# Expert blocks of an eight-layer kernel: tokens scattered into slots ahead of the tile loop, weights copied to fixed buffers, f32 matmuls

## What is computed

```python
probs = softmax(x @ gate_w + gate_b)          # [2048, 8]
topw, topi = top_k(probs, 2); topw = topw / topw.sum(-1)
hid = gelu(einsum('nd,edf->enf', x, w1) + b1)  # w1: [8, 128, 512]
out = einsum('enf,efd->end', hid, w2) + b2     # w2: [8, 512, 128]
final = (out * ew * mask).sum(axis=0)          # weights of the chosen experts
```

## Time and profile before

| | |
|---|---|
| median of 3 runs | 1203.41 us (1202.26 to 1234.69) |
| the profiled execution's own time | 1192.77 us |
| its span | 1190.6 us |
| busy: TensorE / VectorE / ScalarE / GpSimd | 846.7 / 674.1 / 507.5 / 226.8 us |
| mean granted clock of TensorE | 0.819 of full |
| the chain that ended last | TensorE 44%, VectorE 17%, issue 10%, ScalarE 10%, GpSimd 8%, unknown queue 5%, DMA 3% |
| DMA | 32.98 MB, 28 GB/s on average |

### The profile page before, as it was taken

One profiled execution on the slowest core, in us unless ns is written; L12 is line 12 of the kernel. 1 busy time (PEld: TensorE's weight loads), 2 busy tenths in 40 slices (PEclk: granted clock), 3 DMA queues, 4 the chain that ended last, 5 costly groups with the idle time before them and its releaser, 6 DMA issues.

```text
span 1190.6 us, 17358 instructions
## 1 busy us (share of the span) xinstructions
PE 846.7 (71%) x5666; PEld 481.4 (40%) x5666; DVE 674.1 (57%) x1340; ACT 507.5 (43%) x1061; POOL 226.8 (19%) x208
## 2 busy tenths in 40 slices
PE   4599644888825547898878888878784787574784
PEld 2377434666614331111111111111564565374663
DVE  6734767111157768669999999960626311574112
ACT  1110431433316353458888888884233233211332
POOL 2000014465511200000000000000302464101562
PEclk9799756899967765559999999995795699785798
DMA  6100210111120000000000000000203111101113
GB/s 161 46 1 1 72 35 10 35 43 41 41 80 1 0 1 1 1 1 1 1 1 1 1 1 1 1 1 1 71 1 106 27 41 37 35 1 35 39 43 93
DMA packets 35946, 32.98 MB, mean 28 GB/s; under 512 B 6898, under 2 KB 28738, under 8 KB 35874
## 3 DMA queue, kind: packets, MB, share of 16 engines
q1 hardware_dynamic: 30434, 20.82, 6.1%
q0 software_dynamic: 5440, 11.15, 3.7%
HBM read 22.18 MB, written 9.76 MB: 27 GB/s over the span
## 4 chain that ended last, share of the span: by engine, by line
PE 44%; DVE 17%; issue 10%; ACT 10%; POOL 8%; another core or an unknown queue 5%; DMA 3%; SPq 2%; DVEq 0%; POOLq 0%; ACTq 0%
PE psum L1331 12%; PE psum L1319 9%; ACT arena L1383 6%; POOL results L891 4%; POOL arena L883 3%; DVE arena L1298 2%; DVE stats L158 2%; PE psum L1283 2%; PE psum L217 2%; PE psum L916 2%; PE psum L934 2%; PE psum L1449 1%; DVE xn L186 1%; PE psum L282 1%
## 5 line engine op out<-in xcount | busy, mean ns | idle before, releaser
L1298 DVE TENSOR_REDUCE arena<-psum 128x2 f32<-128x1024 f32 x256 | 300.2, 1219 | 48.8 <-PE psum L1283 47.4
L1383 ACT ACTIVATE arena<-psum 128x512 f32<-128x512 f32 x512 | 264.6, 604 | 108.5 <-PE psum L1319 108.4
L1319 PE MATMUL psum<-arena 32*128 32x512 f16 x512 | 130.0, 425 | 60.7 <-ACT arena L1383 59.5
L1018 ACT ACTIVATE arena<-psum,e_b 128x128 f32<-128x128 f32 x340 | 96.4, 370 | 157.2 <-remote 120.3
L1331 PE MATMUL psum<-arena 128*32 128x512 f32 x1024 | 157.0, 690 | 0.0
L1145 DVE TENSOR_TENSOR arena<-psum,arena 128x128 f32 (+1 forms) x85 | 24.8, 292 | 206.1 <-remote 148.6
L1283 PE MATMUL psum<-arena 32*128 32x512 f16 x512 | 122.1, 429 | 12.1 <-DVE arena L1298 9.1
L1319 PEld LDWEIGHTS psum<-arena 32*128 32x128 f16 x512 | 30.3, 92 | 247.8 <-ACT arena L1383 217.3
L970 PE MATMUL psum<-arena,expert_w 128*128 128x128 f16 x1020 | 99.5, 239 | 35.2 <-ACT arena L1018 31.3
L981 PE MATMUL psum<-expert_w,arena 128*128 x680 | 104.6, 299 | 2.3 <-issue 1.3
L891 POOL DMA_INDIRECT results<-arena x85 | 83.6, 984 | 92.2 <-DVE arena L1145 77.2
(11 more groups left out here) (246 smaller groups left out, 1112.5 us busy)
## 6 DMA issues: line engine op xcount, KB each, us to landing
arena<-results SPq DMA_DIRECT2D x16, 256.0 KB, 4.1
tokens<-arena SPq DMA_DIRECT2D x6, 512.0 KB, 3.2
arena<-in_L_attn_b_w_dram SPq DMA_DIRECT2D x1, 2048.0 KB, 8.5
arena<-in_L_ffn_W_dram SPq DMA_DIRECT2D x1, 2048.0 KB, 9.4
arena<-tokens,arena POOLq DMA_INDIRECT x85
results<-arena POOLq DMA_INDIRECT x85
x<-in_L_attn_a_x_dram SPq DMA_DIRECT2D x2, 512.0 KB, 5.3
out_dram<-x SPq DMA_DIRECT2D x1, 1024.0 KB, 5.1
```

The source lines that it names most:

```text
L1018: last = nc.scalar.activation(self.hT[:, p, c, :], ps[:, 2 + p, c * P:(c + 1) * P], self.func, bias=self.ew.b1[:, c:][:, bass.ds(at, 1)])
L1298: v.tensor_reduce(self.mx[:, h % 2, keys, qt, 2 * pair:2 * pair + 2], core.psum[:, 2 * slot:2 * slot + 2, :], AX.X, ALU.max).then_inc(self ...
L1319: nc.tensor.matmul(core.psum[:, 4 + tile % self.SCORE_BANKS, :], self.kT[rows, g, at:at + P], self.qT2[rows, h % 2, :], start=True, stop=T ...
L1383: nc.scalar.activation(self.prob[:, k % self.PROBS, j, :], core.psum[:, 4 + tile % self.SCORE_BANKS, :], ACT.Exp).then_inc(self.prob_in, 1)
```

## The change

The tokens are no longer gathered tile by tile. A DRAM buffer `slots` of 40 x 128 rows takes the place of `tokens`. It is cleared once at the start. As soon as the slots are known (L1089), GpSimd scatters the normalised tokens to it, 128 rows per indirect DMA, 16 x top of them. When all have landed, SP loads the tiles in order with plain DMAs, in groups of 1, 2, 4, 4, ... tiles. GpSimd keeps the scatter of the results.

Tokens and weights stay f32, and the splits into halves are gone. Each expert's w1, b1 and w2 lie side by side in `expert_w` (EW = 1028 columns). For each tile VectorE loads the column of its expert into a register and copies those 1028 columns into one of four fixed buffers (`own`), from which TensorE and ScalarE read at fixed addresses. The first layer becomes four f32 matmuls, and the transposes one in f32. The bias b2 leaves the loop: TensorE multiplies the transposed weights per expert (`whT`) by b2 laid out in blocks, four matmuls of 32 x 128 by 32 x 512, and VectorE adds that to x before the loop. For the blocks, b2 is loaded 16 times for each expert set, so the small loads are 18 for each set. VectorE's and ScalarE's loops are written out for all tiles, and the weights of the second set are loaded once, behind the softmax block's last use of `expert_w`.

```diff
+EW = FF + FC + FC * D
@@ Weights.sync
-        self.e0.load_w2(sp)
+        self.e0.load(sp)
...
-        for e in (self.e0, self.e1):
-            e.bias_to_rows(sp)
...
+        sp.wait_ge(self.blank_in, 1)
+        sp.dma_start(self.slots.rearrange("(t p) d -> p t d", p=P),
+                     self.blank[:, :].unsqueeze(1).to_broadcast([P, 40, D])).then_inc(self.slots_clear, 16)
@@ called in LinearAttention.vector in place of split_biases
+    def bias_blocks(self, dve):
+        core, v = self.core, self.core.nc.vector
+        core.vstep(v.tensor_reduce(self.of_row[:, :], self.ident[:, :].rearrange("p (t e) -> p t e", e=NE), AX.X, ALU.add))
+        core.vstep(v.tensor_reduce(self.of_tile[:, :], self.of_row[:, :].rearrange("p (g j) -> p j g", j=4), AX.X, ALU.add))
+        for e in (self.e0, self.e1):
+            dve.wait_ge(e.small_in, e.small_all)
+            v.tensor_tensor(e.b2_blocks[:, :, :], e.b2_rows[:, :].unsqueeze(1).to_broadcast([P, 4, D]),
+                            self.of_tile[:, :].unsqueeze(2).to_broadcast([P, 4, D]), ALU.mult).then_inc(e.blocks_in, 1)
@@ ExpertWeights
+        loads = [(self.gate[:, :], d["gate"]), (self.gate_b[:, :], d["gate_b"].partition_broadcast(P))]
+        loads += [(self.b2_rows[NE * t:NE * (t + 1), :], d["b2"]) for t in range(T)]
...
+    def load(self, sp):
+        d, parts = self.from_dram, self.parts
+        sp.dma_start(parts[:, :, 0:FF], d["w1"].rearrange("e p f -> p e f")).then_inc(self.weights_in, 16)
+        sp.dma_start(parts[:, :, FF:FF + FC], d["b1"].rearrange("p (e c) -> p e c", e=NE)).then_inc(self.weights_in, 16)
+        for e in range(NE):
+            sp.dma_start(parts[:, e, FF + FC:].rearrange("p (c d) -> p c d", c=FC),
+                         d["w2"][e].rearrange("(c p) d -> p c d", p=P)).then_inc(self.weights_in, 16)
@@ Experts.sync
+        sp.wait_ge(self.scattered, 16 * self.top * T)
+        rows = self.slots.rearrange("(t p) d -> p t d", p=P)
+        for q, (first, stop) in enumerate(self.groups):
+            if q >= 2:
+                sp.wait_ge(self.tile_in[q % 2], 16 * (q // 2))
+            sp.dma_start(self.sorted[:, first:stop, :], rows[:, first:stop, :]).then_inc(self.tile_in[q % 2], 16)
@@ Experts.gpsimd
+        pool.wait_ge(w.slots_clear, 16)
+        pool.wait_ge(self.slotted, 1)
+        for k in range(self.top):
+            for t in range(T):
+                at = k * T + t
+                pool.indirect_dma_start(out=self.slots[:, :],
+                                        out_offset=bass.IndirectOffsetOnAxis(ap=self.slot_int[:, 0, at:at + 1], axis=0),
+                                        in_=core.xn[:, t, :], in_offset=None).then_inc(self.scattered, 16)
@@ Experts.tensor, step s
+                nc.tensor.transpose(ps[:, p, 0:P], self.sorted[:, t, :], w.ident[:, :]).then_inc(core.filled[p], 1)
...
+                pe.wait_ge(self.copied, t + 1)
                 for c in range(FC):
-                    for i, (of_w, of_x) in enumerate(((0, 0), (0, 1), (1, 0))):
-                        last = nc.tensor.matmul(ps[:, 2 + p, c * P:(c + 1) * P],
-                                                w1[:, of_w, c * P:][:, bass.ds(column[t], P)], self.xgT[:, p, of_x, :],
-                                                start=(i == 0), stop=(i == 2))
+                    last = nc.tensor.matmul(ps[:, 2 + p, c * P:(c + 1) * P], own[:, c * P:(c + 1) * P],
+                                            self.xgT[:, p, :], start=True, stop=True)
...
-                nc.tensor.matmul(ps[:, 4 + p, 0:D], w.ones_rows[:, :], brows[:, bass.ds(at, D)],
-                                 start=False, stop=True).then_inc(core.filled[4 + p], 1)
@@ Experts.vector
+        for g, turn in enumerate(self.bias):
+            xs = core.x[:, 4 * g:4 * g + 4, :]
+            core.result(dve, turn)
+            v.tensor_tensor(xs, xs, ps[:, turn.bank, :].rearrange("p (t d) -> p t d", d=D),
+                            ALU.add).then_inc(core.emptied[turn.bank], 1)
+        dve.wait_ge(self.ew.weights_in, self.ew.weights_all)
+        dve.wait_ge(self.tables_in, 1)
+        def take_weights(t):
+            at = dve.value_load(self.tile_at[0:1, 0, t:t + 1], min_val=0, max_val=(NE - 1) * EW)
+            v.tensor_copy(self.own[:, t % self.HELD, :], self.ew.all[:, bass.ds(at, EW)]).then_inc(self.copied, 1)
+        take_weights(0)
+        for s in range(self.tiles + 3):
+            t = s
+            if t < self.tiles:
...
+                self.result(dve, 0, p, m)
+                v.tensor_copy(self.xgT[:, p, :], ps[:, p, 0:P]).then_inc(core.emptied[p], 1)
+            t = s - 3
+            if t >= 0:
...
+                self.result(dve, 2, p, m)
+                v.tensor_scalar(self.y[:, t, :], ps[:, 4 + p, 0:D], self.places[:, 1, t:t + 1], None,
+                                ALU.mult).then_inc(core.emptied[4 + p], 1)
+            t = s + 1
+            if t < self.tiles:
+                take_weights(t)
```

More of the change, by code:

```diff
@@ L373, in vector @@
         v.tensor_copy(w.ident16[:, :], w.ident[:, :]).then_inc(w.ident16_in, 1)
-        w.e0.split_biases(dve)
-        w.e1.split_biases(dve)
+        w.bias_blocks(dve)
         for b in range(B):
@@ L809, in __init__ @@
             meanwhile.take_banks()
+        (self.turn,) = core.turns(1)
+        self.bias = core.turns(4)
         self.base = list(core.uses)
@@ L814, in __init__ @@
             core.uses[i] += (tiles + 1 - i % 2) // 2
-        self.tokens, self.results = w.tokens, w.results
+        self.slots, self.results = w.slots, w.results
+        self.groups = [(0, 1), (1, 3)] + [(t, min(t + 4, tiles)) for t in range(3, tiles, 4)]
         self.results_before = list(w.results_before)
@@ L1150, in vector @@
+        for turn in self.bias:
+            core.moved(dve, turn)
         for g in range(4):
```

260 lines of the change are left out of this document (79 added, 181 removed).

## The result

The changed kernel takes 1136.1 us (median of four runs, 1117.6 to 1151.0) against 1203.5 before: a ratio of 0.935, 95% interval 0.920 to 0.951. Medians and ranges in this document are over all runs, ratios and their intervals over the fast ones alone (the two medians by themselves give 0.944). The forecast was 1192, range 1173 to 1225. The sign was right, the size far off: the gain is 67 us where 11 were forecast.

The account below looks back on a forecast made before the run. The prediction took the expert loops to be bound by a round of loop, ScalarE and TensorE. +10.6 + 30.0 - 50.4 - 1.2 = -11.0 us gave 1192 from 1203.4, range 1173 to 1225.

Parts of the forecast that it names:

- Start: Start of the kernel: VectorE waits for 36 small loads instead of 8 before its first eviction L379, +10.6 us.
- Ahead of the loops: Before each expert loop: scatters and first load delay the first transpose, less 1.58 for L1042; +15.8, +5.7, +8.5, sum +30.0 us.
- the upper bound: Scatters ahead of the loops: each of 16 beside VectorE's work waits for one operation of 0.29; +4.6 us.
- The cover: Ahead of each loop: scatters and loads hide place search, table product and bias matmuls; closest in top1b, 23 us against 25.
- The step of the loops: Expert loops: pace of 3.16 us set by a round of loop, ScalarE and TensorE; 2.40 after, sum -50.4 us.
- The size of TensorE's step: Full steps of the expert loops: TensorE alone needs 2.31 us, with W1 and W2 at 1.08 each.
- The first steps: Start of each expert loop: run-up costed at nothing, first full step 4.2 us at the low clock.
- Rival (a): Expert loops: VectorE's copy stands behind GpSimd's issue in every step; round 2.50, +7 us, 1199; chance 0.25.
- (b): Expert loops: VectorE becomes the bound, copy 1.21 and behind GpSimd's issue; round 3.06, +48 us, 1240; chance 0.12.
- (d): Expert loops: unrolling brings nothing, step stays at 3.16; +55 us, 1247; chance 0.04.
- (e): The forecast itself: loop step 2.31 to 2.45, 1.27 per scatter; 1192, range 1180 to 1206; chance 0.46.
- (c): Scatters run back to back without gap, -18.6 us, 1173; or added loads don't hold VectorE, -10.6, 1181; chance 0.13.

Follow-up runs that it names:

- experiment 5: Two runs on the changed kernel: W2 reading weights through a register's address, 1153.7 us; a bf16 matmul of 3 rows of zeros behind W2, 1156.5 us.

## Why the prediction was wrong, step by step

*Start.* Forecast +10.6, measured +7.2, under the low end of +8.7. The 16 loads of a set are issued in 5.40 and 5.91 us, 0.34 to 0.37 each instead of 0.40, and the last lands about 1.5 us behind its issue instead of 3.2. SP's queue and landings:

```profile
17.72 5.40 SPq L690 DMA_DIRECT2D e_b_rows<-in_L_attn_b_b_dram  x16
...
24.02 5.91 SPq L690 DMA_DIRECT2D e_b_rows<-in_L_ffn_b_dram  x16
...
31.10 0.69 DVE L657 TENSOR_TENSOR e_b_blocks<-e_b_rows,of_tile 128x512 f32<-128x512 f32 x1 [6.08 <-DMA e_b_rows<-in_L_ffn_b_dram]
```

*Ahead of the loops.* Right: 1.27 per scatter, -1.58 for L1042, and +6.1 and +8.9 in the two top1 blocks where +5.7 and +8.5 were forecast. In top2 +18.5 came instead of +15.8. Of this 0.3 is the way from the slots to the first scatter, 0.8 instead of the 0.5 that was read off a gap between the end of an issue and its landing. Most of the rest is what the upper bound had named: scatters beside VectorE's table products are slow, here the first, the fourth and the fifth (1.97), beside the products L1020 and L1032; the second and third, also beside products, take 1.03 and 1.06:

```profile
187.40 2.30 POOL L826 DMA_INDIRECT slots<-xn,arena  x1 [165.19 <-DVE arena L1014]
...
192.71 1.96 POOL L826 DMA_INDIRECT slots<-xn,arena  x1 [0.30 <-issue]
```

The cover was thinner than reckoned, and in top2, not in top1b. TensorE's four bias matmuls, priced at 8.0 us, take 2.09; in top2 they lie at 214.73 to 216.8. But VectorE's additions that wait for them start at 219.35, 223.53, 227.79 and 232.00, each let go by "remote", while 32 scatters go out back to back. Behind the first weight copy (233.07 to 233.76) VectorE is idle for 1.27 us until it copies the first transposes at 235.03; had the last addition come later by more than that, it would have held the loop.

*The step of the loops: the step that failed.* "It is set by a round of loop, ScalarE and TensorE" was argued from two engines that both looped and both waited for "remote", and from a tail without either. But in that tail the gathers end as well, and with them GpSimd's issuing without rest. That was the cause: 0.5 us of the 3.15 are TensorE's ends seen late beside GpSimd's issues (2.58 with the hardware loops but a calm GpSimd, 3.0 without hardware loops but a crowded one), and only 0.1 the loops. The rows for it were there: GpSimd's 2.54 us of issues per tile against TensorE's 2.5 left it no rest, and was dismissed as "just under the 3.16". For the outcome this mattered little, since both theories let the loss vanish. That it did was luck: the change happened to remove the gathers too.

*The size of TensorE's step.* This is the term that was mis-sized: 2.31 forecast, 1.89 measured. W1 and W2 were priced at 1.08 each from the earlier trace rows; with fixed addresses and between f32 neighbours they take 0.89, which is 0.38 of the 0.42, and the transpose 0.11 instead of 0.15. Of W2's 0.19 the runs explain 0.10 (experiment 5); the rest is open, and so is why the f16 W1 took 1.14. Over 73 steps the 2.40 that was taken against 1.93 is 34 of the 43 us that the loops gained beyond the forecast.

*The first steps.* Forecast: 4.2 us for the first full step, at the low clock. In top2 it took 1.89 (238.98 to 240.87), as the clock had risen ahead of it (W1 2.08, 1.57, then 1.06). This and the ends of the blocks make, by subtraction, the other 9 us.

*VectorE.* The copy takes 0.70 (forecast 0.69) and its step fits (its sum of 0.05, 0.7, 0.69 and 0.29 is 1.73, not 1.75). Rival (a) fell: at 255.14 GpSimd issues for 0.96 and the copy runs beside it from 255.23 for 0.70. Over all 85 copies the median is 697 ns; the mean issue of a result's scatter rose to 995 ns from 984. Of the lock that the Trainium skill describes (SBUF — State Buffer, section "SBUF: two separate sides") the loop thus shows little: single issues of up to 1.38 us and no copy over 0.87. With a memset of GpSimd beside it the copy takes 1.64 us, longer by 0.95 where the memset takes 0.97. The same page of the Trainium skill says in "Who interferes with whom" that whoever issues first gets the shared ports and the other fully blocks. The trace agrees with the blocking; who came first it does not show, as it has the copy's start 0.12 us ahead of the memset's (253.40 and 253.52). Rivals (b) and (d) fell with the copy's 0.70 and the step's 1.93, and so did the step of 2.31 to 2.45 of (e), the forecast itself; of (c), nothing came.

*What was not forecast at all* is the softmax loop's -20.9 us in the profiled pair, an effect of the clock and not of the change. The range had no room for it in either direction. It is not what put the result outside: without it the change still gains some 55 us, which from 1203 is 1148.

## What to carry to other kernels

Before a wait is put down to a loop or an engine, look at what else ends where the wait ends, and make the experiment that removes only the suspect. Leave GpSimd rests in a long row of indirect DMAs when other engines hang on TensorE's signals, or move what it issues to SP, as here: beside SP's transfers nothing was lost. Price a matmul from rows whose neighbours and addresses are like those that it will have, and compare two kernels without the stretches whose clock rises by chance.

## What was not expected of the hardware

- Beside indirect DMAs that GpSimd issues with little rest, VectorE and ScalarE see TensorE's matmuls end late: by 2.2 to 2.8 us in the kernel before, by up to 15 us beside 32 scatters in a row. With all gathers first a step reaches 10.5 us. Beside the first 9 of a row nothing is late, nor beside transfers by SP or a memset on GpSimd.
- Four f32 matmuls of 128x128 take 0.89 us between f32 neighbours and 0.99 ahead of a bf16 matmul of 3 rows; with their addresses from a register they take 0.89 as well. Twelve f16 ones with such addresses took 0.68 us at first and then 1.14.
- An indirect scatter's issue grows from 0.96 to between 1.96 and 2.30 us beside some of VectorE's products with both inputs in SBUF, and hardly (1.03, 1.06) beside others.
- For identical instructions the granted clock of the softmax loop rose from 1.2 to 2.4 GHz 45 us behind its start in one execution and 125 in another, worth 33 us.
